# A six-block decoder on one core: last norm of the first stage on ScalarE, and a new order of the parts in the self-attention pass

## The reference, cut to what matters

```python
x = x + attn0(layernorm(x))        # values, k, q: projection, LayerNorm over 256, one head; + its own input
x = x + xattn0(layernorm(x), ctx)  # q * r,  r_t = 0.9 r_{t-1} + ctx_t * ctx_t
x = x + moe0(layernorm(x))         # top-1 router over 8 experts; a token over capacity keeps its normed row
x = x + attn1(layernorm(x))        # 16 heads of width 16, LayerNorm over each head of q and k, softmax, w_proj
x = x + xattn1(...); x = x + moe1(...)
```

## Time and profile before

| | |
|---|---|
| Median of three runs | 2872.43 us (2864.74 to 2880.53) |
| The profiled execution | 2876.24 us, its span 2874.5 us |
| Mean granted TensorE clock | 0.926 of full speed |
| PE busy | 2397.5 us, 83% of the span |
| DVE busy | 1971.9 us, 69% |
| ACT busy | 1444.4 us, 50% |
| POOL busy | 1335.4 us, 46% |

### The profile page before, as it was taken

The page is one execution under the profiler, slowest core; times in us unless marked ns, Lnnn a source line. Parts: engine busy times, 40 slices in busy tenths (PEclk is TensorE's granted clock), DMA queues, the critical chain, the costliest instruction groups (busy, mean ns, idle before and its releaser), DMA issues. The chain is left out here.

```text
span 2874.5 us, 49242 instructions
## 1 busy us (share of the span) xinstructions
PE 2397.5 (83%) x16164; PEld 1881.5 (65%) x16164; DVE 1971.9 (69%) x4760; ACT 1444.4 (50%) x2778; POOL 1335.4 (46%) x1248
## 2 busy tenths in 40 slices
PE   5888888579999579999999999878999885998670
PEld 3666666469999546566565665547888774997560
DVE  4888888556565357878888888745777775765563
ACT  3666666345555247777777777753444341222110
POOL 5777777544443255444344454403656553002545
PEclk9999999889999878999999999889999997999885
DMA  2222212152121000001000010003333343444665
GB/s 69 59 74 59 74 60 63 47 153 95 63 84 40 25 18 30 27 30 31 30 30 30 27 34 23 23 25 127 103 115 117 111 147 118 140 140 152 205 199 157
DMA packets 208168, 226.68 MB, mean 79 GB/s; under 512 B 32254, under 2 KB 194048, under 8 KB 207664
## 3 DMA queue, kind: packets, MB, share of 16 engines
q1 hardware_dynamic: 186352, 177.14, 19.7%
q0 software_dynamic: 20480, 46.39, 5.1%
q10 hardware_dynamic: 1088, 0.00, 0.0%
HBM read 131.99 MB, written 95.49 MB: 79 GB/s over the span
## 5 line engine op out<-in xcount | busy, mean ns | idle before, releaser
L1333 POOL TENSOR_TENSOR f_hm<-f_hm,f_mhalf 128x64 f32<-128x64 f32 x32 | 347.4, 10856 | 2.7
L1513 DVE TENSOR_REDUCE f_nm<-f_raw 128x4 f32<-128x1024 f32 x256 | 312.1, 1219 | 34.0 <-PE f_raw L1634 33.9
L1406 ACT ACTIVATE f_PT<-f_sco 128x1024 f32<-128x1024 f32 x256 | 262.7, 1026 | 81.7 <-PE f_sco L1652 78.7
L2359 POOL DMA_INDIRECT d_pick<-expert_out,e_out_slots x128 | 129.5, 1012 | 319.0 <-DMA expert_out<-d_eo 227.7
L2378 ACT ACTIVATE d_hh<-d_H 128x512 fp32r<-128x512 f32 x78 | 46.7, 598 | 283.9 <-PE d_H L2455 240.7
L1634 PE MATMUL f_raw<-f_k4T,f_q4T 64*128 64x256 f32 x1024 | 140.3, 355 | 37.5 <-DVE f_nm L1513 36.6
L895 ACT ACTIVATE b_hT<-b_H,b_b1r 128x512 f32<-128x512 f32 x128 | 88.3, 690 | 163.5 <-PE b_H L1024 148.5
L1634 PEld LDWEIGHTS f_raw<-f_k4T,f_q4T 64*128 64x128 f32 x1024 | 84.2, 203 | 105.8 <-DVE f_nm L1513 54.3
L1889 POOL DMA_INDIRECT expert_in<-g_xm,e_slots x128 | 130.9, 1023 | 39.7 <-issue 37.0
L1039 PE MATMUL b_O<-b_w2l,b_hTh 128*128 128x256 f32 x512 | 145.8, 285 | 0.0
L1039 PE MATMUL b_O<-b_w2h,b_hTh 128*128 128x256 f32 x512 | 144.8, 283 | 0.0
(11 more groups left out here) (364 smaller groups left out, 7755.6 us busy)
## 6 DMA issues: line engine op xcount, KB each, us to landing
d_xs<-expert_in SPq DMA_DIRECT2D x78, 256.0 KB
expert_out<-d_eo SPq DMA_DIRECT2D x78, 256.0 KB
x_scratch<-a_x SPq DMA_DIRECT2D x64, 256.0 KB, 2.2
b_w<-in_L_ffn_W_dram SPq DMA_DIRECT2D x16, 1024.0 KB
a_x<-in_x_dram SPq DMA_DIRECT2D x32, 256.0 KB
a_cx<-in_ctx_dram SPq DMA_DIRECT2D x32, 256.0 KB
f_x<-x_scratch SPq DMA_DIRECT2D x32, 256.0 KB
f_xr<-x_scratch SPq DMA_DIRECT2D x32, 256.0 KB
```

Of the source, the lines that this page charges most:

```text
L1333: g.tensor_tensor(hm[b % 2][:, :], hm[b % 2][:, :], mhalf[:, :], ALU.pow).then_inc(hroot, 1)
L1406: s.activation(PT[n % 3][:, t, :, :], heads(SCO), ACT.Exp, scale=float(DH) ** -0.5).then_inc(probs_ready, 1)
L1513: v.tensor_reduce(nm[:, t, g * HG:(g + 1) * HG], heads(RAW), AX.X, ALU.max, negate=True)\
L2359: g.indirect_dma_start(pick[b % GR][:, t, c, :], None, ex.eo_d[k], bass.IndirectOffsetOnAxis(ap=ex.out_slots[:, b, t, c:c + 1], axis=0), b ...
```

## The change

First stage: `x2 norm` leaves DVE for ACT, as two activations (one for each 128 tokens) with a scale and a bias column; `passed_by` leaves POOL for ACT in the same form, with a scale that is larger by one, as a new part `x2 pass`. For these columns `root4` on POOL computes three more values. `stats4` gets a wait for `rstd4` of two rounds before, which is long over. In `ORDER`, `route logits` (with `x2 kv`) moves ahead of `in norm`, `ln kT` ahead of `in qk1`, and `ln qT` from the end to before `x2 T`.

Self-attention pass: only `ORDER` changes. `in stats` goes behind `raw 0`; `qk scale` from behind `raw 0` to behind `att 2`; `att 3` ahead of `raw 3`, `att 7` ahead of `raw 7`; `raw 5` ahead of `in v`; `qk split7` behind `raw max1`.

```diff
@@ phase_a @@
         ORDER = (
-            "in stats", "in norm", "x2 kv", "route logits", "sco scores", "x2 sums", "x2 add", "ln sq", "in T",
-            "x2 stats", "sco exp", "route ranks", "in qk0", "ln scale", "sco prT", "in qk1", "ln kT", "x2 norm",
-            "sco inv", "sco att", "x2 T", "sco stats", "in v", "ln qT")
+            "in stats", "x2 kv", "route logits", "in norm", "sco scores", "x2 sums", "x2 add", "ln sq", "in T",
+            "x2 stats", "sco exp", "route ranks", "in qk0", "ln scale", "sco prT", "ln kT", "in qk1", "x2 norm",
+            "sco inv", "sco att", "ln qT", "x2 T", "sco stats", "x2 pass", "in v")
...
             def root4(b):
                 pool.wait_ge(var4, b + 1)
-                root(rs4[b % 2][:, :], mv4[b % 2][:, :, 1], T, None, rstd4)
-
-            def passed_by(b):
-                pool.wait_ge(x2n_ready, b + 1)
-                if b >= 3:
-                    pool.wait_ge(x3_stored[b % 3], 16 * (b // 3))
-                g.tensor_tensor(x3[b % 3][:, :, :], x2[b % 3][:, :, :], x2n[b % 2][:, :, :], ALU.add).then_inc(x3_ready, 1)
+                if b >= 2:
+                    pool.wait_ge(x3_ready, b - 1)
+                stand_alone(pool, pool_passed)
+                step(g.tensor_scalar(minus4[:, :], mv4[b % 2][:, :, 0], -1.0, None, ALU.mult))
+                step(g.tensor_scalar(rs4[b % 2][:, :], mv4[b % 2][:, :, 1], EPS, None, ALU.add))
+                step(g.tensor_tensor(rs4[b % 2][:, :], rs4[b % 2][:, :], mhalf[:, 0:T], ALU.pow))
+                step(g.tensor_tensor(nmr4[b % 2][:, :], minus4[:, :], rs4[b % 2][:, :], ALU.mult))
+                g.tensor_scalar(rsp4[b % 2][:, :], rs4[b % 2][:, :], 1.0, None, ALU.add).then_inc(rstd4, 1)
...
+            def norm4(b):
+                act.wait_ge(rstd4, b + 1)
+                if b >= 2:
+                    wait_full(act, "x2 T", b - 2)
+                for t in range(T):
+                    last = s.activation(x2n[b % 2][:, t, :], x2[b % 3][:, t, :], ACT.Identity,
+                                        bias=nmr4[b % 2][:, t:t + 1], scale=rs4[b % 2][:, t:t + 1])
+                last.then_inc(x2n_ready, 1)
+
+            def passed_by(b):
+                act.wait_ge(rstd4, b + 1)
+                if b >= 3:
+                    act.wait_ge(x3_stored[b % 3], 16 * (b // 3))
+                for t in range(T):
+                    last = s.activation(x3[b % 3][:, t, :], x2[b % 3][:, t, :], ACT.Identity,
+                                        bias=nmr4[b % 2][:, t:t + 1], scale=rsp4[b % 2][:, t:t + 1])
+                last.then_inc(x3_ready, 1)
...
             def stats4(b):
                 dve.wait_ge(x2_ready, b + 1)
+                if b >= 2:
+                    dve.wait_ge(rstd4, b - 1)
                 row_stats(st4[b % 2], mv4[b % 2], x2[b % 3], var4)
-
-            def norm4(b):
-                dve.wait_ge(rstd4, b + 1)
-                if b >= 2:
-                    wait_full(dve, "x2 T", b - 2)
-                    dve.wait_ge(x3_ready, b - 1)
-                normalize(x2n[b % 2], x2[b % 3], mv4[b % 2], rs4[b % 2], x2n_ready)
@@ attention_pass @@
         ORDER = (
-            "in stats", "raw 0", "qk scale", "att 0", "raw 1", "att 1", "out o0", "in norm", "out o1", "raw 2",
-            "att 2", "head var", "in normT", "qk gamma", "out oT", "raw 3", "att 3", "in qk0", "qk high", "in qk1",
-            "out proj", "raw max0", "raw 4", "qk low", "att 4", "raw shift0", "in v", "raw 5", "qk split0", "att 5",
-            "qk split1", "qk split2", "raw 6", "qk split3", "att 6", "qk split4", "qk split5", "raw 7", "qk split7",
-            "att 7", "raw max1", "qk split6", "raw shift1", "att end")
+            "raw 0", "in stats", "att 0", "raw 1", "att 1", "out o0", "in norm", "out o1", "raw 2", "att 2",
+            "qk scale", "head var", "in normT", "qk gamma", "out oT", "att 3", "raw 3", "in qk0", "qk high",
+            "in qk1", "out proj", "raw max0", "raw 4", "qk low", "att 4", "raw shift0", "raw 5", "in v", "qk split0",
+            "att 5", "qk split1", "qk split2", "raw 6", "qk split3", "att 6", "qk split4", "qk split5", "att 7",
+            "raw 7", "raw max1", "qk split7", "qk split6", "raw shift1", "att end")
```

More of the change, by code:

```diff
@@ L156, in phase_a @@
         x2, st4, mv4, rs4 = sbn("x2", 3, [P, T, D]), sbn("st4", 2, [P, T, 6]), sbn("mv4", 2, [P, T, 2]), sbn("rs4", 2, [P, T])
+        minus4, nmr4, rsp4 = sb("minus4", [P, T]), sbn("nmr4", 2, [P, T]), sbn("rsp4", 2, [P, T])
         x2n, x2nT, x3 = sbn("x2n", 2, [P, T, D]), sbn("x2nT", 2, [P, C, S]), sbn("x3", 3, [P, T, D])
@@ L375, in _ @@
             slots({"in stats": rstd1, "in T": residual, "ln sq": rstd2, "ln scale": gain_v, "sco stats": root3,
-                   "x2 stats": root4, "x2 T": passed_by, "route ranks": file_tokens})
+                   "x2 stats": root4, "route ranks": file_tokens})
             for u in range(FR):
@@ L453, in _ @@
                    "ln qT": partial(take_T, "ln qT", qT, gqT, bqT), "ln kT": partial(take_T, "ln kT", kT, gkT, bkT),
-                   "sco exp": exps, "sco prT": take_prT, "x2 kv": square_ctx, "x2 T": take_x2nT})
+                   "sco exp": exps, "sco prT": take_prT, "x2 kv": square_ctx, "x2 norm": norm4, "x2 T": take_x2nT, "x2 pass": passed_by})
         @block.vector
@@ L626, in _ @@
                    "in v": take_v, "sco scores": score_max, "sco inv": invert, "sco att": attend, "sco stats": stats3,
-                   "x2 sums": recur, "x2 add": add2, "x2 stats": stats4, "x2 norm": norm4,
+                   "x2 sums": recur, "x2 add": add2, "x2 stats": stats4,
                    "route logits": route, "route ranks": queue})
```

## The result

The changed kernel takes 2846.82 us (median of 6, 2838.77 to 2852.18); the kernel before, in 6 runs beside it, 2872.23 (2863.61 to 2880.53). The ratio is 0.9912, 95% interval 0.9889 to 0.9935: 25 us faster. I forecast 2820, a gain of 52. The sign and the range held; the size was half.

A forecast was written before the change was run, and what follows sets the result against it. It took a POOL and DVE loop to bound the first stage and PE self-attention; 2876.2 less 34 and 20 gave 2822, or 2818 from the median, stated as 2820 us, range 2788 to 2854.

The forecast's parts named there:

- that loop: First stage: 7.24 us on DVE from norm to `root4`, 8.70 on POOL to the next norm, together the 15.94 us round.
- the next one: First stage: the loop through PE, `in v`, statistics and route was to bind next, at 14.68 us a round.
- the wait for the exponential: Self-attention: the product of `att end` waits 0.41 us for the exponential of `att 7`; the new order was to remove it.
- rival 4: First stage gains more: counted overlaps bring the round to PE's 13.8 us, 60 us saved, 2796 us; chance 0.10.
- 1.2 less than before: First stage: round of 14.7 us in place of 15.94, over 28 rounds 34 us saved.
- The cover is 0.5 us: First stage: ACT's norm ends at 8.6 us after DVE's norm starts, before PE reaches `x2 T` at 9.1.
- about 1 us once, which I leave out: Ends of the first stage: the longer `root4` costs about 1 us once, not counted in the sum.
- 0.67 us a round: Self-attention: gain of the new order, between -0.3 and 1.0 us; over 30 rounds 20 us.
- the waits that go, 0.41 and 0.26: Self-attention: PE's wait for the exponential (0.41 us) and `raw 3`'s wait for DVE's maximum (0.26 us) were to go.
- today it is one in two: Self-attention: TensorE's clock falls in about one round in two, 27.83 us with a fall against 26.83 without.
- Rival 2: Self-attention: the clock falls in every round, 15 us less gain, 2835 us; chance 0.10.

The follow-up runs named there:

- e9: e8 with the first stage's `in stats` and POOL's `rstd1` moved a round ahead, in front of `in v`: 2730.32 us, ratio 0.9699 to the kernel before.
- e4: The changed kernel without the second of POOL's two residual additions (adding `betav`) in the first stage: 2780.31 us, ratio 0.9882 to the kernel before.
- e11: e10 with `in stats` also behind `raw 0` and `qk scale` behind `att 2`: 2764.83 us, one execution.
- e8: The changed kernel with one unneeded 128x256 product on PE behind `att 0` in every self-attention round: 2812.41 us, ratio 0.9807 to the kernel before.
- e5: The kernel before with three unneeded products on PE behind `att 0` in every self-attention round: 2867.99 us, ratio 1.0009 to the kernel before.
- e10: e8 with the old self-attention order except `att 7` ahead of `raw 7` and `qk split7` behind `raw max1`: 2776.69 us, one execution.
- e2: The changed kernel with the old order of the self-attention pass, so only the first stage's change: 2806.44 us, ratio 0.9965 to the kernel before.
- e1: The kernel before with only the new order of the self-attention pass: 2808.61 us, ratio 0.998 to the kernel before.
- e6: The changed kernel, unchanged, run again on another chip: 2847.54 us, ratio 0.9925 to the kernel before.

## Why the prediction was right and wrong

**Right.** The bound before was POOL and DVE; the change breaks that loop, and the next one is norm, PE, `in v`, statistics, route. Its PE part from `in qk0` (306.50) to `sco att` (311.18) took 4.68 us against 4.69 summed (3.95 + 0.3 + 0.44), `root4` 1.93 against 1.9, the norm on ACT 1.09 against 1.02. `e9` confirms the loop by moving a piece out of it: the round fell further than `e4`'s 0.3. ACT did not become the bound. In attention the wait for the exponential went. (A slip without weight: rival 4's 2796 is counted from the profiled execution; from the forecast of 2820 it is 2794.)

**The round of the first stage, "1.2 less than before".** Measured 0.88 less. The term that failed is "the norm on ACT ends at 8.6; PE reaches `x2 T` at 9.1. The cover is 0.5 us". On DVE `x2 add` is the longest thing between the norm and `root4`. In the kernel before, its rows and those of POOL's two residual additions in the same round were:
```profile
318.76 2.12 DVE L542 SCALAR_TENSOR_TENSOR a_x<-a_prod,a_rs,a_x 128x256 f32<-128x256 f32 x2
```
```profile
317.91 1.27 POOL L334 TENSOR_TENSOR a_res<-a_x,a_xn 128x512 f32<-128x512 f32 x1
319.26 1.34 POOL L335 TENSOR_TENSOR a_res<-a_res,a_bv 128x512 f32<-128x512 f32 x1
```
It began 0.85 us into the first addition and took 2.12. In the new order it begins 0.30 into it (306.42 against 306.12) and takes 2.67; `root4` starts 0.5 later, and the cover is used up. Its two instructions one by one:
```profile
306.42 1.25 DVE L562 SCALAR_TENSOR_TENSOR a_x<-a_prod,a_rs,a_x 128x256 f32<-128x256 f32 x1
...
307.59 1.49 DVE L562 SCALAR_TENSOR_TENSOR a_x<-a_prod,a_rs,a_x 128x256 f32<-128x256 f32 x1
```
They end at 307.67 and 309.08, 0.28 and 0.29 us after POOL's two additions end (307.39 and 308.79). In the kernel before the distances are 0.29 and 0.28, in `e4` 0.28. So it is POOL's additions that set the end of `x2 add`: DVE reached it 1.6 us sooner after its norm than before, POOL reached its additions only 1.05 us sooner, and `root4` gained 1.03 (7.24 to 6.21) in place of 1.55. I had counted from a start of `root4` in the old order and subtracted only what left DVE, without asking whether what stayed would run beside other work. `e4` gives that back: 0.3 us, nearly all of the difference. The rest is 0.1 of route and small handshakes. The Trainium skill ("GPSIMD Engine Reference", Specifications) states that GpSimd shares its SBUF interfaces with VectorE, with contention for operations of two SBUF inputs among others; this case's traces agree: 0.88 us for the two operations in `e9`, where they start ahead of POOL's addition (whose own time goes from 1.27 to 1.49), 1.63 behind the start of one addition of POOL, 2.67 behind two.

**The ends of the stage, "about 1 us once, which I leave out".** It was 5 us. From the last maximum to the last slots of the routing it was 558.97 - 536.55 = 22.4 us before and 540.68 - 513.32 = 27.4 after. Where no other sequence fills the time, statistics, `root4`, norm, transpose, logits and route are one chain, so what is added to it counts in full, and it counts once for each of the last two sequences: 1.3 us each from `x2 add` on (12.27 against 10.99 for the last), of which about 0.9 are `root4` and the rest the norm. PE's wait for the last norm, of after (of before it was 4.59), then the clock over PE's products for the last sequence but one, after and before:
```profile
533.82 1.09 PE L652 MATMUL a_bank<-a_ident,a_x2n 128*128 128x128 f32 x4 [6.30 <-ACT a_x2n L453]
```
```profile
524.50:527.20 2.70, 2.70 (x7) 1.98 (x8) 1.31 (x10) 0.00 (x0) 0.00 (x0) 0.50 0.00 0
```
```profile
545.00:547.00 2.00, 1.76 (x10) 1.26 (x9) 1.20 (x10) 0.00 (x0) 1.90 (x4) 1.00 0.09 8
```
Nearly all of the other 2.4 us is there: behind the longer wait for the norm these products run at 0.50, and at 1.00 in the kernel before.

Together: 31 steps x (15.75 - 15.02) = 23, less 5, is 18 us, where I had 34.

**Attention, "0.67 us a round".** The order's own gain was mis-sized: 1.06 us (26.83 to 25.77). I had summed the waits that go, 0.41 and 0.26, and treated the moved statistics as only keeping those gains; `e11` shows 0.6 us for that step.

**Falls of the clock, "today it is one in two" and kept so in the forecast.** This is the step that cost most, 16 us. Rival 2 came true for 19 rounds of 27, and at 1.5 us each, not 1.0. That the total still lies in the range is in part luck: the order's own gain was 10 us larger than forecast and hid part of this. The ledger, from the first reduction to the last: before 831.3 us, less 13 falls at 1.0 is 818; the new order without falls 788.3 (`e8`); so the order is worth 30 us. The kernel after needs 817.8: its falls take 29.5 of that, where before they took 13. 30 + 13 - 29.5 = 13.5 us are left, and 3 of them go in the stretch from there to `g_y`. I had argued over how many holes PE has, when what mattered was where they stand: 0.64 and 0.74 us within 3 us of each other, in every round alike. That `e8` fills one of them and the falls go shows that in this order they need that wait; rounds with both waits and no fall (the first four to six) show that it is not all they need. The Trainium skill ("TensorE: Matmul & The Clock Gate", Part 1) has the low clock as what TensorE returns to without activity; the rows agree (0.50 behind these waits, 1.00 in all of `e8` where one is filled), but in `e5` the same products stand 3 us behind the place where the clock falls, and the falls stay.

**Left open.** What decides between two rounds with the same waits, of which one has a fall and the other none. The old order with three products still has falls, with one product and the new tail (`e10`) it has none; no run has the new tail alone, so how much of that is the tail is not shown. And the 8 us between what `e2`'s trace shows and its medians.

## What to carry to other kernels

When an operation moves to another engine, lay the new round out on a common time axis before pricing the cover: what stays may now run beside another engine's operation and end only after it, and a slack of 0.5 us in 15 does not survive that. Price the drain of a pipeline apart, as one serial chain. And in a pass bound by TensorE, read the granted clock of every round; if it falls in each one, find where in the round it falls and try a product that nobody needs in a wait ahead of that place (behind it, in `e5`, it brought nothing), which here was worth more than the whole change: with it and the statistics moved a round ahead the kernel is at 0.9699 of the time before on its chip, where the change alone is at 0.9912.

## What the hardware showed that I had not expected

- A product of 128x256 of no use to anybody, 0.70 us of a PE that is the bound, made the pass 36 us shorter: the rounds of 27.3 us became 25.8, and the granted clock went from 0.94 to 1.00.
- In the new order nearly all rounds with a fall are 27.2 to 27.3 us, round after round, once the falls begin. In the four traces of this order without a filler (after, `e1`, `e4`, `e6`) the first four to six full rounds have none, with the same waits.
- DVE's two 128x256 operations with two operands in SBUF cost 0.88, 1.63 or 2.67 us: each that starts during one of POOL's 128x512 additions ends 0.28 to 0.29 us after it, in all five read here (after, before, `e4`). Even a DVE operation on 128x16 elements, 0.17 us elsewhere, took 1.19 beside such an addition in `e9` (293.09 to 294.28, the addition ending at 294.25).
- The same kernel's median differs by 53 to 59 us between chips (2813 and 2815 against 2868 and 2872). By the traces the expert part holds some 50 of it and the pass before it up to 6, while the first stage and the feed-forward pass, where the code is the same, agree within about 2 us.
